# Attention of a two-block sequence model: where a pair's second scores stand in TensorE's order

## The reference

```
xn = _modulate(_layernorm(x, ln1_w, ln1_b), shift_a, scale_a)
q, k, v = (xn @ w + b, split into 16 heads of 32 columns, for wq, wk, wv)
scores = einsum('bhqd,bhkd->bhqk', q, k) / sqrt(32)
out = einsum('bhqk,bhkd->bhqd', softmax(scores), v)
x = x + (out @ wo + bo)
```

## Time and profile before

| | |
|---|---|
| time, median of 3 runs | 1930.79 us (1929.43 to 1932.81) |
| time of the profiled execution | 1931.21 us, its span 1929.4 us |
| PE busy | 1877.5 us, 97% |
| DVE / ACT / POOL busy | 64% / 37% / 25% |
| mean granted TensorE clock | 0.992 of full speed |
| attention phase | about 752 to 1230 us of the span |

### The profile page before, as it was taken

One profiled execution on the slowest core, in us unless ns is written; L12 is line 12 of the kernel. 1 busy time (PEld: TensorE's weight loads), 2 busy tenths in 40 slices (PEclk: granted clock), 3 DMA queues, 4 the chain that ended last, 5 costly groups with the idle time before them and its releaser, 6 DMA issues.

```text
span 1929.4 us, 33162 instructions
## 1 busy us (share of the span) xinstructions
PE 1877.5 (97%) x11210; PEld 1568.0 (81%) x11210; DVE 1229.5 (64%) x2058; ACT 716.6 (37%) x2106; POOL 482.7 (25%) x577
## 2 busy tenths in 40 slices
PE   5999999999999999999999999799999999999999
PEld 4778888887888888888888898678888888888887
DVE  5677777766777775888898888555262534436222
ACT  3222232332222223777777777332121212122111
POOL 4243333322222222334444443111010101002000
PEclk8999999999999999999999999899999999999999
DMA  8655444444445543678777777622020211202000
GB/s 288 203 162 180 153 153 157 156 147 142 151 157 163 175 147 109 213 257 262 246 244 260 255 247 259 200 75 88 1 88 23 65 49 38 65 22 85 2 23 22
DMA packets 225200, 276.40 MB, mean 143 GB/s; under 512 B 15308, under 2 KB 144936, under 8 KB 225128
## 3 DMA queue, kind: packets, MB, share of 16 engines
q1 hardware_dynamic: 210624, 232.11, 36.5%
q0 software_dynamic: 12160, 39.14, 6.5%
q10 hardware_dynamic: 2344, 4.25, 0.7%
HBM read 175.29 MB, written 100.14 MB: 143 GB/s over the span
## 4 chain that ended last, share of the span: by engine, by line
PE 79%; DMA 8%; DVE 6%; issue 3%; ACT 2%; POOL 1%; SPq 1%; ACTq 0%; DVEq 0%; POOLq 0%
PE banks L652 29%; PE wide L675 29%; PE banks L1452 17%; DMA turned_squares<-rows 3%; PE wide L1485 2%; DMA rows<-turned_squares 2%; DVE rows L919 2%; PE spare L1508 1%; DMA rows<-gate_bias_rows 1%; ACT rows L805 1%; DVE rows L922 1%; DMA turned_probs<-probs_room 1%; DMA x_tiles<-turned_probs 1%; DVE h L946 1%; ACT probs_room L1647 0%
## 5 line engine op out<-in xcount | busy, mean ns | idle before, releaser
L675 PE MATMUL wide<-weights,h 128*128 128x512 f32 x3072 | 737.5, 390 | 11.3 <-DVE h L946 11.2
L652 PE MATMUL banks<-xn,weights 128*128 128x512 f32 x3048 | 731.3, 390 | 6.9 <-DVE xn L934 6.1
L675 PEld LDWEIGHTS wide<-weights,h 128*128 128x128 f32 x3072 | 575.0, 188 | 138.0 <-DVE h L946 15.4
L652 PEld LDWEIGHTS banks<-xn,weights 128*128 128x128 f32 x3048 | 573.2, 188 | 128.1 <-DVE xn L934 6.5
L816 ACT ACTIVATE rows<-banks,vecs 128x512 f32<-128x512 f32 x256 | 176.4, 689 | 905.7 <-PE banks L652 876.5
L944 DVE CAST h<-rows 128x512 fp32r<-128x512 f32 x256 | 118.3, 462 | 402.3 <-ACT rows L816 379.6
L805 ACT ACTIVATE rows<-rows,mod_tables 128x128 f32<-128x128 f32 x360 | 148.5, 483 | 142.7 <-DMA rows<-turned_squares 142.2
L1452 PE MATMUL banks<-xn,weights 128*128 128x256 f32 (+1 forms) x1524 | 194.9, 289 | 1.0 <-DVE xn L1764 0.9
L1452 PEld LDWEIGHTS banks<-xn,weights 128*128 128x128 f32 x1524 | 188.0, 192 | 5.4 <-DVE xn L1764 1.9
L946 DVE TENSOR_TENSOR h<-rows,h 128x512 fp32r<-128x512 f32 x256 | 186.6, 729 | 8.8
L1452 PE MATMUL banks<-weights,xn 128*128 128x512 f32 x780 | 187.6, 395 | 3.8 <-DVE xn L1811 2.9
(11 more groups left out here) (132 smaller groups left out, 1491.2 us busy)
## 6 DMA issues: line engine op xcount, KB each, us to landing
turned_squares<-rows SPq DMA_DIRECT2D x124, 256.0 KB, 2.8
rows<-turned_squares SPq DMA_DIRECT2D x124, 256.0 KB, 2.9
turned_probs<-probs_room SPq DMA_DIRECT2D x62, 512.0 KB, 3.1
x_tiles<-x SPq DMA_DIRECT2D x98, 256.0 KB, 3.2
x<-x_tiles SPq DMA_DIRECT2D x96, 256.0 KB, 3.5
rows<-gate_bias_rows POOLq DMA_DIRECT2D x64, 256.0 KB, 4.1
probsT_room<-turned_probs SPq DMA_DIRECT2D x64, 256.0 KB, 4.2
x_tiles<-turned_probs SPq DMA_DIRECT2D x64, 256.0 KB, 4.8
```

The source lines that it names most:

```text
L652: last = nc.tensor.matmul(m1_bank(n, c), st.tiles[0](a, k, c), xn[:, parity, b, k, :], start=s == 0, stop=s == len(steps) - 1)
L675: last = nc.tensor.matmul(y_ps[:, tile, :], h[:, c % 2, a, tile * P:(tile + 1) * P], st.tiles[1](b, c), start=c == 0 and s == 0, stop=c == ...
```

## The change

In TensorE's list for `pair_step(n)` the two last items are exchanged: `scores(n, 1)` now stands in front of `weigh(n-1, 1)`. No instruction is added or removed, no wait is changed, and the lists of the other engines stay. For n = 0 there is no `weigh(n-1, 1)`, so the exchange bears on the steps n = 1 to 15.

```
                 if is_first(n):
                     value_bias_product()
+                if is_pair(n):
+                    scores(n, 1)
                 if is_pair(n - 1):
                     weigh(n - 1, 1)
-                if is_pair(n):
-                    scores(n, 1)
```

## The result

The changed kernel is slower: 1941.34 us median (1938.76 to 1944.66, 8 runs) against 1931.88 (1929.43 to 1937.97, 8 runs), a ratio of 1.0046 with a 95% interval of 1.0036 to 1.0055, which is 8.9 us (7.0 to 10.6). The medians differ by 9.5 us; forecast were 9.7. Single executions of one kernel vary by several us, so the profiled one (span 1942.8 us) is read for its places and not for its total: 13.4 us more than the span before, of which 1.3 us lies ahead of the attention and about 0.8 between there and the end of pair 1's keys, ahead of the first exchange.

The account below looks back on a forecast made before the run. TensorE, busy 97% of the span, was taken to bound the kernel. Steps 1 to 14 were to add 8.7 us and the end 1.0, in all 9.7, giving 1940.5 us against the runs' median, with a range of 1937.5 to 1944.8.

Parts of the forecast that it names:

- scores wait for the exponentials: Steady pairs: exponentials end as the slot begins, so the earlier scores start after ACT's hand-over, 0.05 us lost.
- given back in the keys block: Steady pairs: with keys later, VectorE's first two low parts are ready in time and 0.22 us of hidden waiting goes.
- net, steady pair: Each steady pair: stall of 0.88 us less 0.22 given back, 0.66 slower; twelve such pairs make 7.9.
- transfer waits of two second weighings: Pairs 0 and 1: waits for turned probabilities before the second weighings, 1.0 us together, could be covered.
- The stall: Before the next pair's keys: PE waits for the now exposed value copy, 0.83 to 0.93 us, taken as 0.88.
- The pace: Steady pairs: VectorE's first two low parts hold the fourth and fifth key product, a hidden wait of 0.22 us.
- rival A: Steady pairs: the 0.22 us is not VectorE's, nothing is given back; 3.1 us more, 1943.6; chance 0.13.
- Pair 14: Keys behind step 14: stall of 0.88 us less 0.42 given back, 0.46 slower.
- The end: Last step, SyncE's queue: the load of probabilities goes 1.54 us later and delays the store by 1.0, bounds 0 to 1.5.
- Rival B: TensorE's clock falls at each new stall, 2.6 us each: 36 us on top, 1977; chance 0.03.
- Rival C: Not slower: VectorE's chain sets the true pace and the stall fills hidden waits, 0.60 us a pair; 1929.8; chance 0.04.
- Rival D: Another chain: ACT late for low parts or transfers collide; 1.4 us per 0.1 a pair, 1944.7 with 0.3; chance 0.08.

Follow-up runs that it names:

- the banks: Changed kernel with the two value banks exchanged: 1933.66 us, ratio 1.0002; the kernel before with the same exchange of banks: 1933.23 us, 1.0005.
- The memsets: Three small VectorE memsets ahead of tile 1's row maxima: added to the kernel before 1934.86 us, 1.0005; added to the changed kernel 1943.38 us, 1.0049.
- the earlier parts: Kernel before with the second key product's high part (ScalarE) and low part (VectorE) moved earlier: 1930.95 us, ratio 0.9994.
- undoing the order: Changed kernel with exchanged value banks and, in SyncE's last steps, the store of probabilities ahead of the load: 1932.15 us, ratio 0.9997.
- last step only: Kernel before with scores and weighing exchanged in the last step (n = 15) alone: 1934.11 us, ratio 1.0006.

## Why the prediction was right

| step of the forecast | forecast | measured |
|---|---|---|
| scores wait for the exponentials | 0.05 | 0.05 (921.35 to 921.40) |
| scores' start to the keys' start | 3.28 to 3.38, taken 3.33 | 3.38 (921.40 to 924.78) |
| given back in the keys block | 0.22 | 0.25 (12.00 to 11.75) |
| net, steady pair | 0.66 | 0.68 (28.05 to 28.73) |
| net, pair 14 | 0.46 | about 0.8 |
| net, steps 1 to 14 together | 8.7 | 9.4 |
| transfer waits of two second weighings | covered | covered |
| the end, SyncE's store later | 1.0 | 1.3 to 1.9 (5 profiles) |
| the end, stretch to pair 15's first weighing | 1.0 | 1.2 (means of 5 and 6 profiles) |
| total | 9.7 | 9.5 by medians, 8.9 (7.0 to 10.6) by the ratio |

The parts measured in traces, 9.4 and 1.2, add up to 10.6, at the upper edge of the interval of the whole. Each was forecast a little low, so that 9.7 came as near as it did to 9.5 and 8.9 is in part luck.

**The stall** is shown, not only argued: the trace names its releaser, and taking the dependence away through the banks removes it whole. It was 0.93, the upper bound of the forecast: the hand-over from the copy to the keys took 0.14, where the one to the scores takes 0.05.

**The pace.** That the steady pair before was held 0.22 us by VectorE was read from the difference between two keys blocks, since no wait was listed there. The memsets confirm it from one side and the earlier parts from the other. Without this step the forecast would have been rival A's, 3.1 us longer. The Trainium skill ("Perfetto Trace Analysis", section "Tensor Engine Instruction") says that a matmul's end in the profile is estimated from its size and not observed; the trace agrees, since PE stood as busy for all of a block that was 0.22 us too long.

**Pair 14** was the mis-sized term. The forecast gave it the steady pair's 0.05 in front of the scores. Step 14 stands outside the hardware loop, and there the exponentials come late already in the kernel before: they end at 1169.33 + 0.21 = 1169.54, 0.25 after the slot has begun, where in the steady pair the two fall together.

```profile
1169.29 0.30 PE L1508 MATMUL spare<-probsT_room,x_tiles 128*32 128x128 f32 x2
1169.33 0.21 ACT L1647 ACTIVATION_READ_ACCUMULATOR probs_room<-wide,att_negmax 128x1 f32 x1
```

So this could have been read ahead. In the changed kernel its scores waited for them. These are PE's two starts:

```profile
1180.28 1.56 PE L1485 MATMUL wide<-xn 32*128 32x128 f32 x48 [0.26 <-ACT probs_room L1647]
1183.72 11.75 PE L1452 MATMUL banks<-xn,weights 128*128 128x256 f32 x96 [0.87 <-ACT x_tiles L1632]
```

So the 0.42 came back in the keys as forecast (11.75 for 12.20), but 0.26 was lost ahead of the scores and 0.06 more in the stall. The lateness begins one item of ScalarE's list earlier, at L1623, the high parts of the next pair's x, which wait for the values: they start 6.11 us after the 36 matmuls in step 14 and 5.83 in the steady pair. What makes that difference was not tried.

**The end.** The mechanism was right, the load ahead of the store in SyncE's queue: the load came 1.54 later against the start of the stretch, as forecast (9.59 to 11.13), and undoing the order put the store back at its old place. Its size was not: the forecast let the load hold the queue for 0.99 as before, and it held it for 1.28 to 1.93, so that the store came 1.3 to 1.9 later and not 1.0. Of that, 1.2 on average reached the weighing. Why the load takes the queue longer, and what takes up the rest, was not tried. One profile would not have shown it in the stretch: the changed kernel's own has 22.35, inside the spread of those without the exchange.

**Rival B.** All fourteen windows with a stall at the keys (0.81 or 0.87 us of idle) had clock 1.00 in the changed kernel's profile. The Trainium skill's rule on short idle times between groups of matmuls ("TensorE: Matmul & The Clock Gate", section "A second HAM failure mode: psum-queue depth-cycling") did not act at this length and spacing. **Rival C** needed 0.60 us of hidden waiting a pair; the keys block gave back 0.25. **Rival D** showed in pair 14, and in the last step as the longer wait for L1811, which stays hidden.

## What to carry to other kernels

Work between a producer and the next user of its buffer hides the copy between them. Before two independent steps of the busiest engine are exchanged, ask what each one's end releases and what stood behind it as cover: here 16 small matmuls released a 0.60 us copy, and the 1.49 us of scores behind them were its cover. If the order has to change, change who shares the bank.

On an engine that is busy by the profile all the time, compare the same block in different iterations: 11.78 against 12.00 us told which other engine set the pace, and that a stall elsewhere would be given back in part.

## What the runs showed of the hardware

After the idle of 2.70 us before pair 0's second scores the changed kernel's scores still ran at full pace (1.56 us as listed), and the clock fell only during the keys behind them: the first product of 12 matmuls took 2.63 us, where 1.47 is usual. In the kernel before, 3.22 us of idle had the scores themselves at the low level. So the clock fell in both, but at different places behind the wait; what decides the place is not shown. PE in the changed kernel:

```profile
776.65 1.56 PE L1485 MATMUL wide<-xn 32*128 32x128 f32 x48 [2.70 <-ACT probs_room L1647]
778.14 2.63 PE L1452 MATMUL banks<-xn,weights 128*128 128x256 f32 x12
```

A fall also came behind a shorter wait, but not every time. In the last step PE waits 2.08 us for L1811 in all seven kernels with the exchange there, at clock 1.00 up to then. The 12 matmuls of 512 columns behind it took 2.97 to 2.99 us at clock 1.00 in three profiles (changed, exchanged banks, last step only). In the other four they took 4.26 to 4.58, at a mean clock of 0.61 to 0.67. What that cost stayed hidden under the wait for the transfer. Waits of 0.81 us every 28.73 us left the clock at 1.00.

A hand-over from ScalarE to TensorE took 0.05 us for the scores and 0.14 for the keys, in the same pair and in every steady pair; what makes the difference was not tried.
